# Stage weights loaded one stage ahead, and masked sums from three products with the halves of v added by POOL

## The reference

```
smask[i, j] = 1 where (i & j) == 0, else 0          # 256 x 256
scores = (q @ k.T) * scale * smask
a = softmax(scores)                                  # a masked pair counts exp(0 - max)
att = a @ v ; h = layernorm(h + att @ Wo + bo) ; h = layernorm(h + gelu(h @ W1 + b1) @ W2 + b2)
```

## Time and profile before

| | us |
|---|---|
| median of three runs (4094.0 to 4099.04) | 4095.8 |
| the profiled execution | 4093.98 |
| its span, from the first to the last instruction | 4092.1 |
| PE busy | 3362.9 (82% of the span) |
| PEld busy | 2345.6 (57%) |
| DVE busy | 2512.2 (61%) |
| ACT busy | 1836.8 (45%) |
| POOL busy | 1057.8 (26%) |
| mean granted clock of PE | 0.901 |

### The profile page before, as it was taken

How to read it: one execution, slowest core, us unless ns; L and a number is a source line. 1 busy time by engine, 2 the same in 40 slices (tenths; PEclk the granted TensorE clock), 3 DMA queues, 4 the chain that set the end, 5 groups by cost and what they waited for, 6 DMA issues and landing times. The chain is left out here.

```text
span 4092.1 us, 68321 instructions
## 1 busy us (share of the span) xinstructions
PE 3362.9 (82%) x25711; PEld 2345.6 (57%) x25711; DVE 2512.2 (61%) x6468; ACT 1836.8 (45%) x3001; POOL 1057.8 (26%) x1362
## 2 busy tenths in 40 slices
PE   5999999999999999996768586777566659997996
PEld 3666666666666666665668254556354424444674
DVE  4865875775775875874510698886685741115663
ACT  1565565565565565664534552222232213332443
POOL 1324324324324324322454110000201320004321
PEclk8999999999999999998789786998776669997997
DMA  5423534434433534430155100000000000004430
GB/s 134 117 71 98 116 73 99 115 73 100 115 73 97 117 74 99 116 91 1 41 160 181 47 1 0 1 0 1 6 1 5 1 29 0 0 0 110 94 81 26
DMA packets 177020, 262.06 MB, mean 64 GB/s; under 512 B 19950, under 2 KB 149230, under 8 KB 159694
## 3 DMA queue, kind: packets, MB, share of 16 engines
q1 hardware_dynamic: 152494, 140.93, 12.3%
q10 hardware_dynamic: 19656, 107.37, 12.0%
q0 software_dynamic: 4544, 9.38, 0.7%
HBM read 184.67 MB, written 72.19 MB: 63 GB/s over the span
## 5 line engine op out<-in xcount | busy, mean ns | idle before, releaser
L870 DVE TENSOR_REDUCE enc_mx<-psum 128x2 f32<-128x512 f32 (+1 forms) x1152 | 755.6, 685 | 155.7 <-PE psum L550 153.0
L1036 ACT ACTIVATE enc_e<-psum 128x1024 f32<-128x1024 f32 (+1 forms) x768 | 580.3, 808 | 400.4 <-PE psum L571 309.3
L550 PE MATMUL psum<-enc_ks,enc_qs 80*128 80x128 bf16 (+1 forms) x3072 | 459.5, 253 | 69.4 <-DVE enc_mx L870 55.2
L571 PE MATMUL psum<-enc_qs,enc_ks 83*128 83x256 bf16 (+1 forms) x3072 | 380.3, 249 | 29.6 <-DMA enc_qs<-enc_turned_max 21.0
L550 PEld LDWEIGHTS psum<-enc_ks,enc_qs 80*128 80x128 bf16 x3072 | 221.6, 99 | 190.5 <-DVE enc_mx L870 110.4
L584 PE MATMUL psum<-enc_e,enc_v 128*32 128x256 f32 (+1 forms) x6144 | 330.7, 333 | 0.0
L571 PEld LDWEIGHTS psum<-enc_qs,enc_ks 83*128 83x128 bf16 x3072 | 258.2, 98 | 67.8 <-DMA enc_qs<-enc_turned_max 21.4
L584 PEld LDWEIGHTS psum<-enc_e,enc_v 128*32 128x32 f32 x6144 | 160.6, 109 | 161.3 <-ACT enc_e L1036 50.8
L2781 PE MATMUL psum<-ter_h,par_s 128*128 128x512 f32 x512 | 224.9, 593 | 2.4 <-DVE ter_h L2832 1.6
L640 PE MATMUL psum<-par_layerr,enc_hidden 128*128 128x128 f32 x1536 | 191.6, 279 | 16.2 <-DVE enc_n_rows L915 16.2
L640 PEld LDWEIGHTS psum<-par_layerr,enc_hidden 128*128 128x128 f32 x1536 | 182.4, 194 | 26.9 <-DVE enc_n_rows L915 21.2
(11 more groups left out here) (531 smaller groups left out, 7235.3 us busy)
## 6 DMA issues: line engine op xcount, KB each, us to landing
enc_qs<-q_pieces ACTq DMA_DIRECT2D x234, 192.0 KB
enc_ks<-k_pieces ACTq DMA_DIRECT2D x234, 192.0 KB
k_pieces<-enc_pieces SPq DMA_DIRECT2D x240, 128.0 KB, 2.0
moe_wb<-moe_w SPq DMA_DIRECT2D x39, 512.0 KB
q_pieces<-enc_pieces SPq DMA_DIRECT2D x144, 128.0 KB, 2.0
enc_qs<-q_pieces SPq DMA_DIRECT2D x54, 192.0 KB
enc_ks<-k_pieces SPq DMA_DIRECT2D x54, 192.0 KB
rope_qs<-q_pieces ACTq DMA_DIRECT2D x39, 192.0 KB
```

The lines of the kernel that those rows point to most:

```text
L550: last = T_.matmul(p1[f % 2][:, i * kw:(i + 1) * kw], qs[0:KEYED, slot, h, j * P:(j + 1) * P], ks[0:KEYED, slot, h, 0:kw], start=True, sto ...
L571: last = T_.matmul(p2[ch][:, g], ks[0:SCORED, slot, 4 * T + g, ch * P:(ch + 1) * P], qs[0:SCORED, slot, 4 * T + g, 0:n], start=True, stop= ...
L870: V.tensor_reduce(mx[:, u % 2, j * HEADS + h0:j * HEADS + h0 + n], p1[f % 2].rearrange("p (h k) -> p h k", h=n), AX_X, ALU.max)\
L1036: A.activation(e_of(T, ch), p2[ch], ACT.Exp, scale=HD ** -0.5).then_inc(s_e, 1)
```

## The change

**Rooms.** `build` allots three tiles outside the stages: room a for s3, s5 and s7, room b for s6, room c for s4 and s8, each as wide as its widest. Before a stage is run, the `load_stage` of the next one is made in its room, and SP starts that transfer in the stage before the one that uses it: s3 in the experts, behind s2 and ahead of the fillings; s4 in the delta rule's inputs; s5 in FP4; s6 in linear attention, ahead of the wait for the cut bias; s7 in ternary; s8 in rope attention, ahead of the rows of bits. s1 and s2 are loaded as before. Users wait for the same semaphores as before.

**Masked sums.** POOL adds the halves of v over the keys into a new tile `v_both`, both sequences of a group at once (`add_halves`, 128 x 288 elements), 48 times in all: before the first layer ahead of `cut_maxima`, in each odd sequence that has a group after it (behind the root, where there is one), and in the feed-forward part behind `residual1` of the last group. `masked_sum` waits for it and takes three products in place of four: one with `v_both` for the first half of the queries, and two as before for the second half.

```diff
--- before.py
+++ after.py
@@ -267,6 +267,7 @@
         v = sb("v", [P, SLOTS, JT, HEADS, 32])
+        v_both = sb("v_both", [P, SLOTS, HEADS, VW])
         mx = sb("mx", [P, 2, JT * HEADS])
...
         cut = sb("cut", [P, JT, P], BF16)
@@ -286,7 +287,7 @@
         s_stored, s_loaded = [sem(f"pieces_stored{i}") for i in range(2)], [sem(f"pieces_loaded{i}") for i in range(SLOTS)]
-        s_vp, s_v = sem("vproj_ready"), sem("v_moved")
+        s_vp, s_v, s_both = sem("vproj_ready"), sem("v_moved"), sem("v_halves_added")
         s_p1, s_mx = sem("scores_ready"), sem("max_taken")
...
         s_nm, s_nmm, s_nml = sem("max_turned"), sem("max_moved"), [sem(f"max_loaded{i}") for i in range(2)]
@@ -444,6 +445,12 @@
+            def add_halves(layer, nxt, g):
+
+                pool.wait_ge(s_v, at(layer, GROUPS, g + 1, nxt))
+                s = SEQ_G * g % SLOTS
+                G.tensor_tensor(v_both[:, s:s + SEQ_G], v[:, s:s + SEQ_G, 0, :, 0:VW], v[:, s:s + SEQ_G, 1, :, 0:VW], ALU.add).then_inc(s_both, 1)
+
             def first(layer, nxt, g):
...
                     cut_pieces(layer, nxt, g, w)
@@ -455,6 +462,7 @@
             first(0, 0, 1)
+            add_halves(0, 0, 0)
             cut_maxima(0, 0, 0)
...
             def close(k):
@@ -486,8 +494,11 @@
                             residual2(layer - 1, GROUPS - 1)
-                    elif m:
-                        N1.root(pool, at(layer, GROUPS, m - 1))
+                    else:
+                        if m:
+                            N1.root(pool, at(layer, GROUPS, m - 1))
+                        if m + 1 < GROUPS:
+                            add_halves(layer, 0, m + 1)
                 residual1(layer, GROUPS - 2)
...
                     if g:
@@ -501,6 +512,8 @@
                         residual1(layer, GROUPS - 1)
+                        if not last:
+                            add_halves(layer, 1, 0)
                     if g >= 2 and not last:
...
                     if last:
@@ -586,12 +599,11 @@
             def masked_sum(layer, u):
-                pe.wait_ge(s_v, at(layer, GROUPS, u // 2 + 1))
-                for j in range(JT):
-                    for ch in range(JT):
-                        last = T_.matmul(misc[:, j * HEADS * VW:(j + 1) * HEADS * VW].rearrange("p (h v) -> p h v", v=VW), zero[:, ch, j * P:(j + 1) * P],
-                                         v[:, u % SLOTS, ch, :, 0:VW], start=(ch == 0), stop=(ch == 1))
-                last.then_inc(s_u, 1)
+                pe.wait_ge(s_both, at(layer, GROUPS, u // 2 + 1))
+                rows = [misc[:, j * HEADS * VW:(j + 1) * HEADS * VW].rearrange("p (h v) -> p h v", v=VW) for j in range(JT)]
+                T_.matmul(rows[0], zero[:, 0, 0:P], v_both[:, u % SLOTS], start=True, stop=True)
+                T_.matmul(rows[1], zero[:, 0, P:2 * P], v[:, u % SLOTS, 0, :, 0:VW], start=True, stop=False)
+                T_.matmul(rows[1], zero[:, 1, P:2 * P], v[:, u % SLOTS, 1, :, 0:VW], start=False, stop=True).then_inc(s_u, 1)
...
                 pe.wait_ge(s_ot, at(layer, 32, 2 * u + half + 1))
@@ -1807,6 +1818,7 @@
             W.start(sp)
+            c.ahead["s3"].start(sp)
             spare = EXPERTS * SLOT_T
...
                          c.params["moe_fill"][spare:].rearrange("(p r) w -> p (r w)", p=P)).then_inc(s_filled, 16)
@@ -2445,7 +2457,7 @@
         def _(sp):
-            W.start(sp)
+            c.ahead["s6"].start(sp)
             sp.wait_ge(s_cut, 5)
@@ -3596,9 +3608,9 @@
-    def __init__(self, c, ctx, name):
+    def __init__(self, c, ctx, name, room=None):
         self.layout, width = c.layouts[name]
-        self.sb = ctx.enter_context(c.nc.sbuf_tensor(f"par_{name}", [P, width], F32))
+        self.sb = room[:, 0:width] if room is not None else ctx.enter_context(c.nc.sbuf_tensor(f"par_{name}", [P, width], F32))
         self.sem = c.sem(f"par_{name}_loaded")
@@ -3658,7 +3670,15 @@
         base = 0
-        for stage in (encoder, experts, delta_rule, fp4_network, linear_attention, ternary_network, rope_attention, fft_mix):
+
+        c.ahead, rooms = {}, {}
+        stages = ((encoder, None, None), (experts, "s3", "a"), (delta_rule, "s4", "c"), (fp4_network, "s5", "a"), (linear_attention, "s6", "b"),
+                  (ternary_network, "s7", "a"), (rope_attention, "s8", "c"), (fft_mix, None, None))
+        for stage, following, room in stages:
+            if following:
+                if room not in rooms:
+                    rooms[room] = sb("weights_" + room, [P, max(layouts[f][1] for _, f, r in stages if r == room)])
+                c.ahead[following] = load_stage(c, ctx, following, rooms[room])
             base = stage(c, base)
```

More of the change, by code:

```diff
@@ L1166, in sb @@
         def sb(n, shape, dt=F32): return ctx.enter_context(nc.sbuf_tensor("rope_" + n, shape, dt))
-        W = load_stage(c, ctx, "s7")
+        W = c.ahead["s7"]
         scored = PIECES + 3
@@ L1221, in _ @@
         def _(sp):
-            W.start(sp)
+            c.ahead["s8"].start(sp)
             for slot in range(SLOTS):
@@ L1638, in sb @@
         def sb(n, shape, dt=F32): return ctx.enter_context(nc.sbuf_tensor("fft_" + n, shape, dt))
-        W = load_stage(c, ctx, "s8")
+        W = c.ahead["s8"]
         freq_t, mix, y = sb("freq_t", [P, 2, P]), sb("mix", [P, P]), sb("y", [P, 2, GROUP])
@@ L2181, in sb @@
         def sb(n, shape, dt=F32): return ctx.enter_context(nc.sbuf_tensor("fp4_" + n, shape, dt))
-        W = load_stage(c, ctx, "s4")
+        W = c.ahead["s4"]
         HBLOCKS, XBLOCKS, WBLOCKS = TILES * FF4 // BLK, GROUP // BLK, 9 * P // BLK
@@ L2208, in _ @@
         def _(sp):
-            W.start(sp)
+            c.ahead["s5"].start(sp)
         @block.gpsimd
@@ L2413, in sb @@
         def sb(n, shape, dt=F32): return ctx.enter_context(nc.sbuf_tensor("lin_" + n, shape, dt))
-        W = load_stage(c, ctx, "s5")
+        W = c.ahead["s5"]
         KD, PAIR = KVH * HD, KVH * VW * HD
@@ L2736, in sb @@
         def sb(n, shape, dt=F32): return ctx.enter_context(nc.sbuf_tensor("ter_" + n, shape, dt))
-        W = load_stage(c, ctx, "s6")
+        W = c.ahead["s6"]
         silu = sb("silu", [P, 2, GROUP])
@@ L2751, in _ @@
         def _(sp):
-            W.start(sp)
+            c.ahead["s7"].start(sp)
         @block.gpsimd
@@ L2914, in sb @@
         def sb(n, shape, dt=F32, ctx=ctx): return ctx.enter_context(nc.sbuf_tensor("del_" + n, shape, dt))
-        W = load_stage(c, ctx, "s3")
+        W = c.ahead["s3"]
         q_all, k_all, ka_all, dec_all = (sb(n, [P, SEQS, S]) for n in ("q_all", "k_all", "ka_all", "dec_all"))
@@ L2971, in _ @@
         def _(sp):
-            W.start(sp)
+            c.ahead["s4"].start(sp)
         @block.gpsimd
```

## The result

| | before | changed |
|---|---|---|
| median of 20 runs each | 4099.6 us | 4110.7 us |
| lowest, highest | 4092.1, 4108.5 | 4101.4, 4118.4 |
| ratio to before, 95% interval | | 1.0026 (1.0017 to 1.0034) |

The account below looks back on a forecast made before the run. The encoder was taken as bound by TensorE (PE), later stages as opening with a wait for weights. From 4093.98 us, 27.8 (weights) and 1.3 (encoder, -22.4 + 21.1) came off: 4064.9, as median 4066.7, said as 4066; range 4044 to 4074.

Parts of the forecast that it names:

- The weights: Stage heads: loads issued one stage earlier save 28.2 us, less 0.4 in linear attention, together 27.8 us (bounds 22 and 31).
- that term: FP4 head: its 576 KB of weights, loaded a stage earlier, let the stage start 4.3 us sooner.
- Linear attention: Linear stage: the tiny bias queues behind s6, so the 2.98 us gain is gone and 0.4 us more.
- One product less: Encoder masked sums: three products for four save 0.275 us, 96 times, 26.4 us; 22.4 left (bounds 13 and 27).
- even ones: full gain: Even encoder sequences: PE goes on with scores whose inputs are long ready, so the shorter product's gain is kept in full.
- the odd ones: Odd encoder sequences: PE already waits for ACT in 17 of 36, over 0.27 us in 11; 3.4 us of gain lost.
- The new sum on POOL: Odd encoder sequences 3 to 13: a 0.79 us sum starts 65 ns ahead of L897 and delays it, 36 x 0.585 = 21.1 us.
- the six that were: Encoder trace of before: all six L897 meeting a running L437 are held, as at 606.39, 1.17 us instead of 0.29.
- The clock: Rival, odd sequences: longer PE waits drop the clock to 1.2 GHz, +1.7 us each, 61 us, 4128; chance 0.03.
- a layer of 291 to 292 us: Sign that the forecast is right: a middle encoder layer lasts 291 to 292 us.

Follow-up runs that it names:

- both orders above: Bias sent ahead of s6 instead of behind it, against the kernel with the sum ahead of POOL's root: 4063.9 us, ratio to before 0.9881.
- the kernel without a sum: Changed kernel with early weights and three products but no sum on POOL, the first product reading one half of v: 4064.5 us, ratio to before 0.9891.
- the second chip: The changed kernel run again, unaltered, on another chip against the kernel before: ratio 1.0013.
- the sum moved: Changed kernel with POOL's sum moved ahead of its root: 4101.4 us, ratio to before 0.9897; again on another chip 4091.6 us, ratio 0.9885.

## Why the prediction was wrong

**The weights: right.** Heads and first users came as said, 28.2 us of transfers, and the measured gain of the early weights alone is 33 us (23 to 43) against 27.8. The profile shows one term less: FP4's first user starts 4.3 us earlier in its stage and the stage is only 0.6 shorter, its PE work having taken 135.8 us in place of 132.3 (granted clock 0.73 against 0.74). Of the twelve profiles with early weights four have a stage of 216 us and eight one of 220 to 221; one of each was looked at, with 132.0 and 136.4 us of PE and the same DVE and ACT time. So that term is kept in some executions and lost in most; that the clock takes it is likely and not shown. Linear attention was right in mechanism, place and size: the first projection 9.2 us behind the barrier, forecast 8.7 to 9.7. The Trainium skill, DMA: Bandwidth & Descriptors, "Queues, rings and completion order", says that SP's transfers share one row of rings and that each DMA engine takes descriptors in ring order; by it the tiny bias stands behind s6 where s6 is issued first, and both orders above agree, with 5.2 us and 1.9.

**One product less: mechanism right, size too large.** Forecast were 22.4 us. With the sum out of the way, an odd sequence is 15.20 - 14.95 = 0.25 us shorter, nearly the whole 0.275; an even one 14.05 - 13.89 = 0.16. The step "even ones: full gain" failed: the trace has a new wait of PE there, 0.13 us for DVE's maxima, that was not there before. And the odd ones kept more than I allowed, because I had misread how often PE stands there for ACT already. By the idle times of the trace of before it is in 14 of the 36 odd sequences up to the eleventh, not 17, and for over 0.27 us in 7, not 11; five of the seven are the first odd sequence of a layer. For seven odd and seven even ones in each of six layers that is 17 us; the medians give 13 (4114.7 - 4101.4).

**The new sum on POOL: right in length and hold.** 0.835 us (forecast 0.79), starting 0.06 us ahead of the division product (forecast 0.065), which ends 0.15 us behind it, 22.7 us in all (forecast 21.1). The Trainium skill, SBUF — State Buffer, "Who interferes with whom", has the engine that comes first keep the shared read interface while the other blocks. Kernels that differ in the instruction beside the product agree: it takes 0.29, 0.60 and 0.93 us beside no sum and sums of 0.51 and 0.84. Starting first was not enough by itself, though. In the trace of before 82 products began 0.14 to 0.19 us behind a subtraction of POOL with two operands in SBUF that had 0.06 to 0.10 us left to run, and none was held (timeline):

```profile
485.87 0.25 POOL L416 TENSOR_TENSOR enc_left<-enc_top,enc_cut 128x32 f32<-128x32 f32 x1
...
486.02 0.29 DVE L897 TENSOR_TENSOR enc_att<-enc_num,enc_rec 128x128 f32<-128x128 f32 x1
```

The argument looked only at the six that were. Where between a POOL instruction of 0.25 us and one of 0.51 the hold sets in was not tested.

**The clock: wrong, and it is the step that decided.** I took the encoder for -22.4 + 21.1 and left the clock a chance of 0.03, "against it: 0.98 over the layer in spite of waits of 1 us as at 523.17". That row was the wrong witness. It is a single wait of 0.92 us, and the question was what happens at 1.4; the nearest row below doesn't speak for a wait half as long again. The trace of before had better ones. In the sequences 1 to 14 of its six layers PE stands seven times for 1.3 us or more, for a load or for ACT, and behind three of the seven (1.87, 1.92 and 2.22 us) the clock falls for 3.4 us. One of them (timeline, then busy time by stretch):

```profile
1632.62 0.68 PE L571 MATMUL psum<-enc_qs,enc_ks 83*128 83x256 bf16 x4 [1.87 <-ACT enc_e L1036]
```

```profile
1619.20:1630.70 11.50, 11.22 (x146) 8.49 (x144) 9.53 (x20) 5.61 (x9) 5.32 (x8) 1.00 0.70 213
1633.00:1636.40 3.40, 3.40 (x32) 2.07 (x30) 2.15 (x5) 2.08 (x6) 0.00 (x0) 0.50 0.81 164
```

A mean of 0.98 over a layer hides such stretches. The four without a fall took 1.33, 1.51, 1.59 and 2.16 us. These rows do not say how many of the 36 would fall, but they speak against a chance of 0.03. The rival was well placed (the odd sequences, behind PE's wait for the maxima), its condition (17 of 36) was met with 20 to 26, and its price of 1.7 us was too high: the fall costs 16.40 - 15.58 = 0.8 us in its own sequence. Between the change and the kernel without a sum, on one chip, lie 4112.1 - 4064.5 = 47.6 us; 22.7 are the hold, and the other 25 are put down to the clock, 1.2 us for each of 20 falls, the delay of what follows included. The profiles of the two agree: the encoder takes 48.0 us longer, 39.9 of them in the 36 odd sequences 3 to 13 and 6.7 in the even ones 2 to 14. That rival ended at "slower", as the kernel did.

**The sum by terms:** -33 (weights) - 13 (product) + 48 (hold and clock) = +2 us, against +11 (7 to 14) and, on the second chip, +5 (-1 to +12). Each term has an interval of some 10 us, so they meet.

**A slip beside it.** The stretch of 292 us that I called a middle layer leaves out part of one: from first scores to first scores a layer takes 306 to 308 us before, 310 to 318 changed, 303 to 306 with the sum moved, in most layers. The argument did not use its length, but "a layer of 291 to 292 us" could not be read off as written.

## What to carry to other kernels

Before an instruction is given to POOL, look at what DVE runs in that slot: an instruction of DVE with two operands in SBUF that starts just behind it is late by POOL's remaining time (sums of 0.5 us and more; one of 0.25 us did no harm), while one slot earlier, beside reductions from PSUM, the same sum was free. Where PE already stands for 0.8 us at one place in each round, price a longer stop there with the clock too: here 0.6 us more cost 1.3. And a small transfer that someone waits for goes on a queue ahead of a large one that nobody needs yet.

## What had not been expected of the hardware

PE's clock fell to 1.2 GHz for 3.4 us behind one stop of 1.4 us, where PE had been busy for 12.3 of the 12.7 us ahead of it. Behind stops of 0.74 to 0.81 us at that place it fell in none of the sequences of six profiles; behind stops of 1.37 to 1.45 us it fell in 18 to 26 of 36 and not in the others. Falls differ between executions of one kernel, 20 and 26 of 36. A short instruction of POOL (0.25 us, two operands in SBUF) did not hold DVE's product that began 0.15 us behind it; one of 0.51 us did. POOL's time does not go by elements alone: 128x288 in runs of nine took 0.835 us, 128x416 in runs of thirteen 0.878, 128x144 in runs of nine 0.509.
